# Four-layer graph attention on 1 core: NxN tiles with their columns in another order, block moves in 4 transfers

## The reference

```python
# layers 0 and 1 (additive scores; slopes 0.2 and 0.1; layer 1 has a bias)
h = x @ W
e = leaky_relu((h @ a_src)[:, :, None] + (h @ a_dst)[:, None, :])
out = elu(softmax(where(adj > 0, e, -9e15)) @ h)
# layer 2 (8 heads; edge types from adj)
scores = leaky_relu(q @ k.T / 8 + edge_bias[edges], 0.2)
out = softmax(where(edges > 0, scores, -1e9)) @ v  ->  @ Wp + bp
# layer 3: pairwise features
s = leaky_relu(u[:, :, None, :] + v[:, None, :, :], 0.2);  e = s @ a
out = elu(softmax(where(adj > 0, e, -9e15)) @ hp)
```

## Time and profile before

| | us |
|---|---|
| median of 3 runs | 8914.21 (8890.67 to 8918.11) |
| the profiled execution, its time | 8904.98 |
| its span, first to last instruction | 8903.0 |

### The profile page before, as it was taken

One profiled execution on the slowest core, in us unless ns is written; L12 is line 12 of the kernel. 1 busy time (PEld: TensorE's weight loads), 2 busy tenths in 40 slices (PEclk: granted clock), 3 DMA queues, 4 the chain that ended last, 5 costly groups with the idle time before them and its releaser, 6 DMA issues.

```text
span 8903.0 us, 165380 instructions
## 1 busy us (share of the span) xinstructions
PE 8014.2 (90%) x57777; PEld 3625.0 (41%) x58360; DVE 7412.9 (83%) x11189; ACT 7008.6 (79%) x8204; POOL 1430.5 (16%) x582
## 2 busy tenths in 40 slices
PE   3899998999989999999999989899898998989999
PEld 2534435344353433435334353443534435343352
DVE  3788887988879888798888978888798887988888
ACT  2788786977879778797787878878697786977877
POOL 0301203021030311203012030120302103031000
PEclk7999999999999999999999999999999999999999
DMA  2614416153262523516135171441615326152250
GB/s 73 162 35 113 105 52 158 42 126 87 59 149 51 142 64 75 134 49 161 44 96 122 44 172 35 113 105 51 158 42 124 88 58 149 49 137 71 59 125 19
DMA packets 430042, 822.71 MB, mean 92 GB/s; under 512 B 163874, under 2 KB 221218, under 8 KB 427042
## 3 DMA queue, kind: packets, MB, share of 16 engines
q1 hardware_dynamic: 429090, 810.76, 37.7%
HBM read 76.25 MB, written 4.19 MB: 9 GB/s over the span
## 4 chain that ended last, share of the span: by engine, by line
PE 46%; DVE 16%; issue 14%; ACT 11%; SPq 11%; DMA 2%; DVEq 0%; ACTq 0%; POOL 0%; POOLq 0%
PE psum L822 22%; SPq L388 10%; ACT work L1048 6%; DVE work L1406 5%; PE psum L532 4%; PE psum L699 4%; PE psum L674 4%; PE psum L604 3%; DVE work L1256 3%; DVE work L1284 3%; PE psum L670 2%; ACT work L958 2%; PE psum L527 2%; PE psum L569 1%; PE psum L549 1%
## 5 line engine op out<-in xcount | busy, mean ns | idle before, releaser
L822 PE MATMUL psum<-work,pick 128*32 128x512 f32 x32768 | 3764.0, 598 | 191.6 <-DVE work L1406 160.8
L1048 ACT ACTIVATE work<-spare,ucol 128x1024 f32<-128x1024 f32 x3402 | 3631.2, 1144 | 52.6 <-PE psum L822 48.1
L1406 DVE TENSOR_SCALAR work<-spare,ucol 128x1024 f32<-128x1024 f32 x4790 | 3250.9, 746 | 72.7 <-PE psum L822 56.3
L822 PEld LDWEIGHTS psum<-work,pick 128*32 128x32 f32 x32768 | 976.8, 110 | 2531.0 <-issue 2064.0
L958 ACT ACTIVATE work<-psum,beta 128x1024 f32<-128x1024 f32 x1024 | 1139.5, 1113 | 484.9 <-PE psum L674 379.9
L1256 DVE CUSTOM_DVE_ANT_0 work<-psum,work 128x1024 f32<-128x1024 f32 x1024 | 1230.2, 1201 | 248.8 <-ACT work L958 238.7
L1284 DVE STREAM_TRANSPOSE work<-work 128x1024 f32<-128x1024 f32 x960 | 1190.9, 1241 | 172.7 <-DMA work<-work 104.4
L965 ACT ACTIVATE work<-work,least 128x1024 f32<-128x1024 f32 x1024 | 1172.7, 1145 | 26.3 <-DVE least L1256 26.2
L1487 POOL TENSOR_TENSOR rstd<-rstd,neg_half 128x8 f32<-128x8 f32 x64 | 131.6, 2056 | 4985.9 <-DVE rstd L1195 4985.9
L674 PE MATMUL psum<-x_split,q_hi 128*128 128x512 f32 x2048 | 852.1, 497 | 0.0
L670 PE MATMUL psum<-mask,ident_b 128*128 128x512 bf16 x1793 | 576.1, 392 | 242.6 <-DVE least L1256 209.8
(11 more groups left out here) (167 smaller groups left out, 6945.7 us busy)
## 6 DMA issues: line engine op xcount, KB each, us to landing
work<-work SPq DMA_DIRECT2D x2560, 128.0 KB, 2.4
spare<-work SPq DMA_DIRECT2D x1280, 128.0 KB, 2.4
adj_in<-in_adj SPq DMA_DIRECT2D x128, 512.0 KB, 5.1
q_lo<-adj_in SPq DMA_DIRECT2D x1024, 64.0 KB, 2.0
q_lo<-spare SPq DMA_DIRECT2D x1024, 64.0 KB, 2.0
work<-work SPq DMA_DIRECT2D x1792, 32.0 KB, 1.8
mask<-mask_next SPq DMA_DIRECT2D x16, 2048.0 KB, 9.2
x_in<-in_x SPq DMA_DIRECT2D x16, 256.0 KB, 9.8
```

Source lines behind the costliest of these rows:

```text
L822: mm = pe.matmul(slot[32 * q:32 * q + 32, cols], pick[:, 15 - kk:47 - kk], ring[kk % 4][q][:, cols], start=False, stop=(kk == 15), skip_gr ...
L1048: ins = act.activation(ring[kk % 4][q], v3, ACT.Relu, bias=ucol[:, 4 * T + q, kk:kk + 1])
L1406: ins = dve.tensor_scalar(ring[kk % 4][q], v3, ucol[:, 4 * T + q, kk:kk + 1], 0.0, ALU.add, ALU.max)
```

## The change

Before, the node with number 128b + 32c + j stood in column 128b + 32c + j. Now, in all N x N tiles, column 128b + 32c + q holds node 128b + 4q + c. After DVE's block transposes, partition 32a + q holds, for c = 0 to 3, the rows a of node 4q + c. Such a partition's contents, cut in four, belong on the partitions 4q to 4q + 3, which are neighbours, so one transfer takes 32 source partitions with four times the bytes each and writes all 128 partitions. A move is 4 transfers (a = 0, 2, 1, 3) and not 16; the bytes are the same. The partition of the moved data is the node's own number, so the values need no reordering.

What makes columns now reads every fourth element (`mixed`) and writes in order (`placed`): PE's products for the columns of layers 0 and 1 and for `v3`, ACT's and DVE's parts of `x_split`, POOL's and (element 0) DVE's two conversions of the adjacency.

The last quad of layer 2 and layer 3's tile 7 are transposed by DVE and moved by DMA like the others: the last quad in two halves of two tiles (4 transfers of 256 KB each), behind each other in a third of the `quadT` buffers. PE's turns and DVE's copies of these five tiles go away. In layer 2's beginning, tile 7's product moves from step 0 to step 1, the turn of layer 3's output from step 1 to step 2.

```diff
@@ -53,7 +53,7 @@
-MOVE_DONE = 16 * 16
+MOVE_DONE = 4 * 16
...
@@ -96,13 +96,12 @@
-    uses = [("tile3", 0)] if tail else []
+    uses = []
     for s in range(STEPS2):
         if extra_use(s):
             uses.append(extra_use(s))
-        if tail and s == 1:
+        if tail and s == 2:
             uses.append(("out3", 0))
-        uses += [("tile", n) for n in (2 * s, 2 * s + 1) if not in_quad(n)[3]]
     return uses + [("heads", HP - 1)]
...
@@ -112,7 +111,17 @@
-LAST = numbered([("xT2", 0), ("v3", 0), ("tile3", 0), ("out3", 0)])
+LAST = numbered([("xT2", 0), ("v3", 0), ("out3", 0)])
+
+
+def mixed(nodes):
+
+    return nodes.rearrange("p (b q c) -> p b c q", c=4, q=32)
+
+
+def placed(columns):
+
+    return columns.rearrange("p (b c q) -> p b c q", c=4, q=32)
...
@@ -235,8 +244,8 @@
-        last_rows = [adj_in[:].rearrange("p a b -> p (a b)").bitcast(F32),
-                     work[:, 4:6, :].rearrange("p a b -> p (a b)")]
+        last_blocks = [blocks[MOVED % 2][:, 0:2 * N], blocks[MOVED % 2][:, 2 * N:4 * N]]
+        lastT = [quadT[MOVED % 3][:, 0:2 * N], quadT[MOVED % 3][:, 2 * N:4 * N]]
...
@@ -381,21 +391,20 @@
             def move(dst, src, done):
-                parts = src.rearrange("p (c y) -> p c y", c=4)
-                for turn_ in range(4):
-                    for a in range(4):
-                        c = (a + turn_) % 4
-                        sp.dma_start(dst[32 * c:32 * c + 32, a, :], parts[32 * a:32 * a + 32, c, :]).then_inc(done, 16)
+                for a in (0, 2, 1, 3):
+                    sp.dma_start(dst[:, a, :], src[32 * a:32 * a + 32]).then_inc(done, 16)
 
             def move_quads(g, more, tail):
                 ready(s_moved_a, (g * NT + NT) * MOVE_DONE)
+                if tail is not None:
+                    move_tile(tail, NT - 1)
                 if more:
                     ready(s_xin_free, g + 1)
                     load_x(g + 1)
                     next_adj(g + 1, 0)
                     next_adj(g + 1, 1)
                 for k in range(MOVED):
-                    ready(s_blocks, g * 4 * MOVED + 4 * k + 4)
+                    ready(s_blocks, g * TILES2 + 4 * k + 4)
...
@@ -407,6 +416,11 @@
+                for half in range(2):
+                    ready(s_blocks, g * TILES2 + 4 * MOVED + 2 * half + 2)
+                    if half == 0:
+                        ready(s_pv, g * QUADS + MOVED - 2)
+                    move(lastT[half].rearrange("p (a y) -> p a y", a=4), last_blocks[half], s_last[half])
...
@@ -487,7 +501,7 @@
-            for T in range(NT - 1):
+            for T in range(NT):
                 move_tile(B - 1, T)
...
@@ -533,6 +547,12 @@
+            def columns_from(dst, weights, src=xTa):
+                for c in range(2):
+                    cols = slice(c * HALF, (c + 1) * HALF)
+                    mm = pe.matmul(placed(dst[:, cols]), weights, mixed(src[:, cols]), start=True, stop=True)
+                return mm
+
...
@@ -556,7 +576,7 @@
-                from_xT(score[1], WD[:, 0, :], xT_in[:]).then_inc(s_column0, 1)
+                columns_from(score[1], WD[:, 0, :], xT_in[:]).then_inc(s_column0, 1)
...
@@ -674,11 +694,6 @@
-            def turn_tile(g, it, n):
-                fill(pe, it, ("tile", n))
-                pe.wait_ge(s_probs, g * TILES2 + n + 1)
-                turned(turn_rows(lambda t: probs[n % 4][:, t * P:(t + 1) * P]))
-
...
@@ -702,15 +717,16 @@
-            def pv_last(it, half):
-
-                in_sbuf(pe, it, ("tile", TILES2 - 3 + 2 * half))
-                src = last_rows[half].rearrange("p (b a h i) -> p b a h i", a=4, h=2, i=32)
+            def pv_last(g, half):
+
+                pe.wait_ge(s_last[half], (g + 1) * MOVE_DONE)
+                src = lastT[half].rearrange("p (a b h i) -> p b a h i", a=4, h=2, i=32)
                 cols = slice((NT - 2 + half) * P, (NT - 1 + half) * P)
                 for j in range(NT):
                     for h in range(2):
-                        mm = pe.matmul(outT[F * h:F * h + F, cols], vw[:, (HP - 1) % 2, j, F * h:F * h + F],
-                                       src[:, j, :, h, :], start=(j == 0), stop=(j == NT - 1))
+                        dst = outT[F * h:F * h + F, cols].rearrange("p (a i) -> p a i", a=4)
+                        mm = pe.matmul(dst, vw[:, (HP - 1) % 2, j, F * h:F * h + F], src[:, j, :, h, :],
+                                       start=(j == 0), stop=(j == NT - 1))
...
@@ -735,33 +749,21 @@
-                    if tail is not None and s == 0:
-                        in_sbuf(pe, it, ("tile3", 0))
+                    if tail is not None and s == 1:
                         pv_tile(tail, NT - 1)
-                    if tail is not None and s == 1:
+                    if tail is not None and s == 2:
                         turn_out3(tail, it)
                     if s >= LAG:
                         pv_quad(g, it, (s - LAG) // 2, (s - LAG) % 2, tail)
-                    if not in_quad(n)[3]:
-                        turn_tile(g, it, n)
                     scores(g, it, n + 3, tail)
-                    if not in_quad(n)[3]:
-                        turn_tile(g, it, n + 1)
                 pv_quad(g, it, MOVED - 2, 0, tail)
-                turn_tile(g, it, TILES2 - 2)
                 pv_quad(g, it, MOVED - 2, 1, tail)
-                turn_tile(g, it, TILES2 - 1)
-                pv_last(it, 0)
                 pv_quad(g, it, MOVED - 1, 0, tail)
                 pv_quad(g, it, MOVED - 1, 1, tail)
-                pv_last(it, 1)
+                pv_last(g, 0)
+                pv_last(g, 1)
                 turn_heads(g, it, HP - 1)
 
-
-            def turn_tile3(g, it):
-                fill(pe, it, ("tile3", 0))
-                pe.wait_ge(s_probs3, g * NT + NT)
-                turned(turn_rows(lambda t: probs3[1][:, t * P:(t + 1) * P]))
...
@@ -769,6 +771,7 @@
+                pe.wait_ge(s_moved3, (g * NT + T + 1) * MOVE_DONE)
...
@@ -791,7 +794,7 @@
-                turned(from_xT(turn, G_of(1)))
+                turned(columns_from(turn, G_of(1)))
...
@@ -906,7 +906,7 @@
-                    act.activation(x_split[:], turn, ACT.Copy).then_inc(s_hi_a, 1)
+                    act.activation(placed(x_split[:]), mixed(turn), ACT.Copy).then_inc(s_hi_a, 1)
...
@@ -1236,7 +1236,8 @@
-                    dve.tensor_tensor(x_split[F:P, :], turn[F:P, :], x_split[F:P, :].bitcast(F32), ALU.subtract)\
+                    low = placed(x_split[F:P, :])
+                    dve.tensor_tensor(low, mixed(turn[F:P, :]), low.bitcast(F32), ALU.subtract)\
...
@@ -1273,25 +1274,17 @@
-            def turn_tile(g, it, n):
+            def turn_tile(g, n):
                 k, half, h, moved = in_quad(n)
-                if moved and k >= 2 and half == 0 and h == 0:
+                if k >= 2 and half == 0 and h == 0:
                     dve.wait_ge(s_moved[(k - 2) % 4],
                                 g * (MOVES[(k - 2) % 4] * MOVE_DONE) + (moved_before(k - 2) + 1) * MOVE_DONE)
+                dve.wait_ge(s_probs, g * TILES2 + n + 1)
                 if moved:
-                    dve.wait_ge(s_probs, g * TILES2 + n + 1)
-                    dst = blocks[k % 2].rearrange("p (c b h t i) -> p c b h t i", c=4, h=2, t=2, i=32)
-                    dve.transpose(dst[:, :, :, h, half, :], by_part(probs[n % 4]))\
-                       .then_inc(s_blocks, 1)
-                    return
-                if h == 0 and half == 0:
-                    dve.wait_ge(s_mask_next, g + 2)
-                if h == 0 and half == 1:
-                    dve.wait_ge(s_pv, g * QUADS + MOVED - 2)
-                filled(dve, it, ("tile", n))
-                dst = last_rows[half].rearrange("p (b a h i) -> p b a h i", a=4, h=2, i=32)
-                dve.tensor_copy(dst[:, :, :, h, :], turn.rearrange("p (b a i) -> p b a i", a=4, i=32))\
-                   .then_inc(s_turn_free, 1)
+                    dst = blocks[k % 2].rearrange("p (c b h t i) -> p c b h t i", c=4, h=2, t=2, i=32)[:, :, :, h, half, :]
+                else:
+                    dst = last_blocks[half].rearrange("p (c b h i) -> p c b h i", c=4, h=2, i=32)[:, :, :, h, :]
+                dve.transpose(dst, by_part(probs[n % 4])).then_inc(s_blocks, 1)
...
@@ -1310,7 +1303,7 @@
                 if tail is not None:
-                    copy_tile3(it)
+                    blocks_tile3(tail, NT - 1)
                 leaky(g, 1, flagged)
...
@@ -1462,9 +1450,9 @@
-                pool.tensor_scalar(mask_next[:, t, :], adj_in[:, t % 2, :], float(TYPES - 1), CODE, ALU.min, ALU.mult)\
-                    .then_inc(s_pool, 1)
-                pool.tensor_scalar(no_edge[:], adj_in[:, t % 2, :], 0.0, MASKED, ALU.is_le, ALU.mult)\
+                pool.tensor_scalar(placed(mask_next[:, t, :]), mixed(adj_in[:, t % 2, :]), float(TYPES - 1), CODE, ALU.min,
+                                   ALU.mult).then_inc(s_pool, 1)
```

(1 more changed line is left out.)

## The result

The change is slower. It takes 9089.19 us (median of 4 runs, 9074.39 to 9095.56) beside 8904.28 us for the kernel before in the same job (4 runs, 8890.67 to 8918.11): a ratio of 1.0207, 95% interval 1.0192 to 1.0221. The forecast was 8820 with a range from 8730 to 8950, so the result lies outside it and on the other side. The profiled execution spans 9072.6 us, 170 more than before.

The account below looks back on a forecast made before the run. SyncE's issuing of moves was taken to bound layer 2, PE close behind. 16 x (-4.5 + 1.8 - 1) = -59, -30 for element 0 and +3 at the end made -86 from 8903; forecast 8820 us, range 8730 to 8950.

Parts of the forecast that it names:

- reads with a stride: PE's four strided fp32 products per element: between nothing and 2 us each, taken as nothing; POOL's slower conversions hidden.
- M: Time of a quad's move from ready to landed: 10.7 us, where it was 13.0 before.
- The last tiles by DMA: Layer 2's last quad and layer 3's tile 7: 1.8 us lost, 1 gained per element, 3 lost at program end.
- The body's gain of 72: Layer 2's body: quads every 10.9 us instead of 11.27, gaining 4.5 us per element.
- Issues: Four transfers of a move hold SP for 1.5 to 2.5 us instead of 10, so SP stops being the bound.
- Transfer: DMA engines carry one quad of 2.10 MB in 8.2 us, chosen between 6.7 and 10.4.
- the prediction's own formula: Layer 2's body, limit of the two block buffers: a quad takes at least (M + 9.5) / 2, 10.1 us.
- sign of being wrong: Layer 2's body: the forecast is wrong if quads stay 11.2 us apart.
- PE as the next limit: Layer 2's body without SP's bound: PE comes latest, 10.9 us per quad at 0.965 busy.
- Layer 2, the end: Last product ends 20.7 us after quad 14 is transposed, not 18.9: 1.8 us lost per element.
- The third rival: DMA becomes the bound in layer 2, above all at its end: slower, 8948 us, chance 0.11.
- Layer 2, the start: Layer 3's last tile loses a PE turn: 1 us gained per element; later x and adjacency loads cost nothing.

Follow-up runs that it names:

- e1: The change, but its column products read xT plainly and the readers of PSUM make the order: 8968.83 us, 1.0075 of the kernel before.
- e12: Kernel before with new order, 4-transfer moves and plain product reads, last tiles still turned by PE (output not the reference's): 8884.42 us, ratio 0.9984.
- e6: e1 with each transfer reading a quarter of the columns of all 128 partitions (output not the reference's): 8729.44 us, ratio 0.981.
- e9: The change with only the product xTa times G read plainly, the other column products still strided: 9006.81 us, ratio 1.0119.
- e13: e12, but exp writes layer 2's last four tiles in memory order into quad 12's buffer, so the output is the reference's: 8923.96 us, ratio 1.0019.
- e14: Kernel before with only the product xTa times G reading with a stride (output not the reference's): 8990.95 us, ratio 1.0097.
- e8: e1 with 32 extra products into a free slot while PE waits for quad 14's move: 8968.32 us, ratio 1.0085.
- e10: e1 with each move in 8 transfers of 16 to 64 partitions, alternating between the four source groups: 9276.6 us, ratio 1.0415.
- e11: e1 with each move in 16 transfers of 8 to 32 partitions, cycling through the four source groups: 11966.74 us, ratio 1.3439.
- e2: Kernel before with new order, strided products and 4-transfer moves, last tiles still turned by PE (output not the reference's): 9002.65 us, ratio 1.0113.
- e4: The change with the old column order and old 16-transfer moves, keeping only the last tiles by DMA: 9340.8 us, ratio 1.0486.

## Why the prediction was wrong, and where it was right

The forecast missed by 269 us. Three terms carry it, as differences of medians, and two steps failed: the reads with a stride, taken at nothing, and the time from ready to landed, M, taken as D + 2.5 (D is the time in which the DMA engines carry a quad). The strided reads cost 120 (change less e1). The last tiles by DMA, priced at 16 x (1.8 - 1) + 3 = 16, cost 84 (e1 less e12). The body's gain of 72 didn't come. Together 260.

**Issues: half right.** Four transfers in an empty queue do hold SP shortly (3.24 us for a pair move in element 0, above the forecast's 1.5 to 2.5, against 10.0 before). In layer 2 it is held 7 to 8 us, with earlier transfers in flight.

**Transfer: the step that failed for the body.** D was taken as 8.2 us with "the source seems the tighter side"; it is 9.0. The earlier trace rows already had the old transfers at 230 to 242 GB/s for a full share in this very stage; the wide destination added nothing to that. That alone would not have cost the gain: by the prediction's own formula M would be 11.5 and a quad still 10.5. What failed is M = D + 2.5. From quad 14 transposed (4300.75) to its product (4313.74) lie 13.0 us, the M that the prediction had for before, and (13.0 + 9.5) / 2 = 11.25 is close to the 11.44 us that a quad takes. For each of the five `spare` quads of a layer 2 the median from transposed to landed lies between 12.7 and 14.4 us in the change and between 12.7 and 14.7 before. The prediction's sign of being wrong, quads that stay 11.2 us apart, came. The missing 1.5 us lie at the beginning: quad 13's last transfer lands at 4302.75, 1.8 us behind quad 14's first issue, and these are the 4 us behind the move's first issue, and the next 4 (us, busy times, PEclk, DMA share, GB/s):

```profile
4301.00:4305.00 4.00, 4.00 (x30) 2.36 (x28) 3.90 (x5) 2.37 (x4) 2.44 (x2) 1.00 0.87 137
4305.00:4309.00 4.00, 1.71 (x16) 0.86 (x12) 4.00 (x5) 2.11 (x5) 0.12 (x1) 1.00 0.94 242
```

The engines count as busy for 0.87 of the first stretch and deliver little more than half of what they do in the second; how much of this is the tail of the move ahead no run separates. In e6 the same distance is 8.2 us (D + 2.7) and the body took the 10.9 us per quad that I had forecast. So the reasoning on PE as the next limit fits e6; it rested on a transfer time that no run out of 32 partitions reached.

The Trainium skill, page "SBUF — State Buffer", section on the DMA port swizzle, was weighed in the prediction and its direction then set aside for 243 GB/s: partitions 0 to 31 reach 8 of 16 ports, about 218 GB/s. The trace agrees on the direction (234 GB/s against 381) and exceeds the figure by 7 per cent. By the page's figure the forecast would have been 8864, nearer, and still on the wrong side.

**Layer 2, the end: mechanism right, size off.** With D = 9.0 the formula T + 0.6 + 2D + 1.9 + 1.8 gives T + 22.3; measured T + 22.8. So 3.9 us at this end (4.3 in the mean) instead of 1.8. On top come 5.8 us from the last product to the first pair move; 5.3 go with plain reads, and e9 lays 5.1 of them on the G product. The third rival had named this place and condition (DMA as the bound, above all at the end), had the sign, and gave 8948. It had no term for the reads; e1, without them, is 8969.

**Layer 2, the start: no gain.** The 1 us counted for the turn of tile 7 doesn't show: e12, with PE turns, and e1, without, both have 339 to 340 us over that stage and layer 3, and so has the kernel before.

**Reads with a stride: the step that failed most.** The prediction counted four such instructions per element; there are twelve. Its "between nothing and 2 us each" held for them, and so its own sign, growth by more than 1 us, did not come. PE's groups, after:

```profile
L553 PE MATMUL psum<-xTa,WD 64*128 64x512 f32 x64 | 61.5, 1093 | 1.2 <-ACT xTa L904 1.2
L553 PE MATMUL psum<-xTa,G 65*128 65x512 f32 x64 | 61.1, 1089 | 19.2 <-ACT xTa L1030 19.2
L546 PE MATMUL psum<-spare,lin 64*128 64x512 f32 x64 | 60.5, 1098 | 0.0
L546 PE MATMUL psum<-xTa,G 65*128 65x512 f32 x64 | 56.4, 1036 | 0.0
```

645 and 648 ns became 1093 and 1089, so "fp32 takes columns slowly anyway" was no reason for zero. The two lower rows have no stride at all, and took 748 and 648 ns before: they pay for the clock. The prediction costed an instruction by itself and left out what PE is granted behind it. All in, strided reads cost 7.5 us per element. The upper end of the term, 4 x 2 us, is nearly that, 128 us in the run, but by luck: no row gives the 2 us, and neither the count nor the cause was this. I left it out of the sum and out of the range, and gave it part of a chance of 0.03. The Trainium skill, page "SBUF — State Buffer", its note on cachelines in the section on the DMA port swizzle, says that SBUF serves full bandwidth to accesses within a 16-byte line and that each crossing pays. That agrees with the trace: with a step of 16 bytes every column is in another line, and the product takes 1.69 times as long. The same note gives 4 fp32, which is this step, as how far one can stride for free; that the trace contradicts. I had not weighed it.

**Right:** element 0 gained 32 us (forecast 30), its fourth pair's product starts at 106.46 (forecast 107). The end of the program lost 3 us as forecast (the last product waits 8.6 us for a move). POOL's conversions went from 3.64 to 4.69 us and stayed hidden; ACT's and DVE's strided reads of PSUM cost nothing: x_split's copy takes 1.008 us before and 1.007 after, its subtraction 1.228 and 1.227.

## What to carry to other kernels

When a transfer's issue stops being the bound, what comes next is the time from ready to landed, so price the new transfer in its own shape: here 32 source partitions gave 234 GB/s where 128 gave 381, and in layer 2, with earlier transfers in flight, fewer transfers bought nothing (e12). Put a permutation where ACT or DVE reads PSUM, which was free here, not into the operand that a product streams from SBUF; ACT's exp with steps in SBUF cost 1 us more as well (e13). And price an instruction on PE with the clock that it leaves behind: four instructions that took 1.8 us longer cost some 5 us (82 us in 16 elements, e9).

## What the runs showed that I had not expected

- A product that reads fp32 columns with a step of 16 bytes takes 1.09 us in place of 0.65, and the granted clock then falls from 1.00 to 0.50 for over 12 us although PE is busy without a pause (e14, and the change; not e9, not e1). 85 us of a run of 8900 hang on it.
- Keeping PE busy through a wait of 7 us kept its clock at 1.00 there, and the time was the same: the last products waited for their moves all the same, and layer 3's first products have half clock with the filling and without it (e8, e1).
- Moves of the same bytes in packets of the same size land in 4.1 us out of 128 partitions and in 7.7 out of 32; e6 is 240 us faster than e1. With 16 source partitions a transfer, 202 GB/s at full share; with 8, no more than about 8 packets are under way at once, SP is held for up to 2 us per transfer and the run is a third longer (e10, e11).
- Two edits that cost 98 and 436 us alone cost 185 together (e2, e4, the change), since the half moves cost far less with four cheap issues than with sixteen.
